# The passage from layer 0 to layer 1 in a four-layer graph kernel: halves of x moved up in two queues

## What is computed

```
x = _layernorm(x + _L0_gnn_ref(x, adj, ...), axis=-1)   # hypergraph convolution, 256 -> 512 -> 256
x = _layernorm(x + _L1_gnn_ref(x, adj, ...), axis=-1)   # q k v projection, scores, softmax
x = _layernorm(x + _L2_gnn_ref(x, adj, ...), axis=-1)
x = _layernorm(x + _L3_gnn_ref(x, adj, ...), axis=-1)
```

```
h = jax.nn.relu(hypergraph_conv(x, adj, W1, b1))
h = layer_norm(h, gamma, beta)
y = hypergraph_conv(h, adj, W2, b2)
return y + x
```

## Time and profile before

| | us |
|---|---|
| median of 3 runs (lowest to highest) | 689.02 (687.34 to 689.32) |
| the profiled execution, its own time | 687.93 |
| its span in the profile | 686.1 |
| PE busy | 628.5 (92%) |
| DVE busy | 564.2 (82%) |
| ACT busy | 525.1 (77%) |
| POOL busy | 372.5 (54%) |

### The profile page before, as it was taken

How to read it: one execution, slowest core, us unless ns; L and a number is a source line. 1 busy time by engine, 2 the same in 40 slices (tenths; PEclk the granted TensorE clock), 3 DMA queues, 4 the chain that set the end, 5 groups by cost and what they waited for, 6 DMA issues and landing times.

```text
span 686.1 us, 15857 instructions
## 1 busy us (share of the span) xinstructions
PE 628.5 (92%) x5014; PEld 453.4 (66%) x5014; DVE 564.2 (82%) x1712; ACT 525.1 (77%) x1191; POOL 372.5 (54%) x448
## 2 busy tenths in 40 slices
PE   5899999999999999879999799999999997999993
PEld 4577777777777776546666456665656664778783
DVE  3899988888888886758888858988888987688886
ACT  4667888777777787748888667877777875899995
POOL 1335556665555555756666414444434444798993
PEclk9999999999999999989999899999999999999998
DMA  9672438464544222545454324545454544378873
GB/s 276 182 210 56 88 71 223 82 160 95 140 121 96 63 32 32 93 95 95 91 92 93 61 63 79 105 86 103 84 103 81 105 85 71 69 176 188 183 188 124
DMA packets 174466, 76.14 MB, mean 111 GB/s; under 512 B 122160, under 2 KB 173872, under 8 KB 174384
## 3 DMA queue, kind: packets, MB, share of 16 engines
q1 hardware_dynamic: 164208, 66.34, 41.9%
q0 software_dynamic: 8448, 8.39, 8.3%
q10 hardware_dynamic: 1728, 0.40, 0.3%
HBM read 28.97 MB, written 8.39 MB: 54 GB/s over the span
## 4 chain that ended last, share of the span: by engine, by line
PE 25%; DVE 10%; POOL 6%; DMA 5%; issue 4%; ACT 2%; DVEq 0%; ACTq 0%; POOLq 0%
PE banks L86 8%; PE banks L88 7%; PE banks L87 7%; DVE l_st L1044 4%; DMA xT_lo<-x_halves 3%; POOL x_halves L1130 2%; POOL l_rstd L1069 2%; DMA l_TT_lo<-l_T_lo 2%; POOL l_U L1961 1%; PE banks L1224 1%; PE banks L1554 1%; DVE l_mid_lo L1716 1%; POOL l_T_lo L1758 1%; PE banks L1236 1%; PE banks L1832 1%
## 5 line engine op out<-in xcount | busy, mean ns | idle before, releaser
L1078 ACT ACTIVATE x_resident<-l_pre,l_nmr,l_rstd 128x256 f32<-128x256 f32 x256 | 142.3, 608 | 19.7 <-POOL l_nmr L1072 19.7
L973 POOL TENSOR_TENSOR hq<-hq 128x512 f32<-128x512 f32 x48 | 69.5, 1447 | 94.0 <-ACT hq L690 91.7
L1130 POOL TENSOR_TENSOR x_halves<-x_resident,x_halves 128x1024 f16<-128x1024 f32 x46 | 98.0, 2131 | 25.5 <-DVE l_pre L1307 22.3
L1044 DVE BATCH_NORM_STATS2 l_st<-l_pre 128x6 f32<-128x256 f32 x256 | 93.4, 411 | 0.0
L86 PE MATMUL banks<-Wk_lo,xT_hi 128*128 128x258 f16 (+1 forms) x256 | 84.5, 330 | 0.6 <-DVE l_far_lo L1709 0.3
L87 PE MATMUL banks<-Wk_hi,xT_lo 128*128 128x258 f16 (+1 forms) x256 | 84.5, 330 | 0.0
L88 PE MATMUL banks<-Wk_hi,xT_hi 128*128 128x258 f16 (+1 forms) x256 | 84.4, 330 | 0.0
L1069 POOL TENSOR_TENSOR l_rstd<-l_veps,minus_half 128x4 f32<-128x4 f32 x64 | 70.5, 1102 | 11.8 <-DVE l_veps L1058 6.2
L86 PE MATMUL banks<-W2T_lo,h_hi 128*128 128x257 f16 x256 | 70.8, 277 | 5.3 <-ACT zf L702 4.5
L88 PE MATMUL banks<-W2T_hi,h_hi 128*128 128x257 f16 x256 | 70.9, 277 | 0.0
L87 PE MATMUL banks<-W2T_hi,h_lo 128*128 128x257 f16 x256 | 70.7, 276 | 0.0
(11 more groups left out here) (200 smaller groups left out, 1942.7 us busy)
## 6 DMA issues: line engine op xcount, KB each, us to landing
adj<-in_adj SPq DMA_DIRECT2D x32, 256.0 KB, 3.6
x_halves<-in_x SPq DMA_DIRECT2D x16, 512.0 KB, 4.3
x_resident<-b_half SPq DMA_DIRECT2D x8, 1024.0 KB, 7.7
x_resident<-in_x POOLq DMA_DIRECT2D x16, 512.0 KB, 6.0
out<-x_resident SPq DMA_DIRECT2D x15, 512.0 KB, 3.2
x_resident<-in_L_gnn_W SPq DMA_DIRECT2D x2, 512.0 KB, 5.7
x_resident<-in_L_gnn_Wk SPq DMA_DIRECT2D x1, 768.0 KB, 9.2
xT_hi<-x_halves SPq DMA_TRANSPOSE x48, 3.2
```

Of the source, the lines that this page charges most:

```text
L973: pool.tensor_tensor(hq[:, 0, :], hq[:, 0, :], hq[:, h, :], ALU.add).then_inc(hqs_ok, 1)
L1044: dve.bn_stats(L.st[p][:, j, :], L.pre[p][:, j, :]).then_inc(L.st_ok, 1)
L1078: act.activation(K.x[:, gcols(g, j)], L.pre[p][:, j, :], ACT.Identity, bias=L.nmr[p][:, j:j + 1], scale=L.rstd[p][:, j:j + 1]).then_inc(L. ...
L1130: pool.tensor_tensor(F.xs[p][1], x_group(K, g), F.xs[p][0], ALU.subtract).then_inc(F.x_lo, 1)
```

## The change

ACT: `first_high(0)` stands in the step of group 14 and `first_high(1)` in the step of group 15, both beside `copy_z` of graph 3 of the group before. In the step of group 15 `copy_z` of graph 0 stands ahead of the four `norm_apply`, graph 1 between them, graph 2 behind them, and `squares_high` follows in the next step. POOL: `first_low(0)` and `first_low(1)` stand behind `hidden_power` in the steps of groups 12 and 13. In the step of group 14 `norm_scales` stands behind `hidden_power`. The seam's word 'nnno' puts three steps of layer 1, with the low halves of its groups 2 and 3, ahead of POOL's last step of layer 0, whose work is `norm_scales` of group 15. PE, DVE and SP keep their order, and no instruction is added or taken out.

```diff
-SEAMS_POOL = ('ooooo', 'ooon', 'ooonnn')
+SEAMS_POOL = ('nnno', 'ooon', 'ooonnn')
...
# layer 0, ACT, step
-            if has(-1):
+            if has(-1) and g < G:
                 copy_z(g - 1, 1)
+            if has(-1):
                 copy_z(g - 1, 2)
...
-            if has(-1):
+            if g == G - 2:
+                first_high(0)
+            if has(-1) and g < G:
                 copy_z(g - 1, 3)
+            if g == G - 1:
+                first_high(1)
+            if g == G:
+                squares_high(G - 1)
+                copy_z(G - 1, 3)
...
-            if isinstance(g, int) and g == G - 1:
-                first_high(0)
-                first_high(1)
+            if g == G - 1:
+                copy_z(G - 1, 0)
             if has(-2):
                 norm_apply(K, L, act, g - 2, p, 0)
                 norm_apply(K, L, act, g - 2, p, 1)
+            if g == G - 1:
+                copy_z(G - 1, 1)
+            if has(-2):
                 norm_apply(K, L, act, g - 2, p, 2)
                 norm_apply(K, L, act, g - 2, p, 3)
-            if has(0):
+            if has(0) and g < G - 1:
                 copy_z(g, 0)
                 squares_high(g)
...
# layer 0, POOL, step
-            if isinstance(g, int) and g == G - 2:
-                first_low(0)
-                first_low(1)
...
-            if has(0):
+            if has(0) and g != G - 2:
                 norm_scales(K, L, pool, g, p)
             if has(1):
                 hidden_power(g + 1)
+            if g == G - 2:
+                norm_scales(K, L, pool, g, p)
+            if g == G - 4:
+                first_low(0)
+            if g == G - 3:
+                first_low(1)
```

More of the change, by code:

```diff
@@ L735, in step @@
             once(g, 0, W.high_w2, act)
+            if has(-1) and g < G:
+                copy_z(g - 1, 1)
             if has(-1):
-                copy_z(g - 1, 1)
                 copy_z(g - 1, 2)
```

## The result

The changed kernel takes 685.33 us (median of 11 runs, 682.47 to 687.60), the kernel before 689.02 (11 runs). The ratio is 0.9945, with a 95% interval of 0.9927 to 0.9964: 0.55% faster. The profiled execution took 683.69 us, its span is 681.9, its mean clock 0.988 (before: 687.93, 686.1 and 0.981).

What follows compares the result with a forecast made beforehand. PE was taken as the bound in layer 0 (163.50 of 166.00 us busy), so only its waits could be won: +2.7 + 0 - 0.4 - 2.1 - 2.7 = -2.5 us, 685.4 from 687.93, median 686.5; range 682.6 to 691.3.

Steps and rivals of the forecast that it cites:

- First low half of group 0: Layer 0, behind zrs of group 13: POOL's low half delays DVE's `zn` and `h_lo`; PE loses 2.7 us (bounds 1.0 to 5.3).
- The first step: At zrs of group 13, POOL goes on with the low half until 255.1, so DVE's `zn` is 1.85 us late.
- gets in ahead of `h_lo` 1: POOL's sum of squares (1.32 us) runs between DVE's `h_lo` 0 and `h_lo` 1, which then ends near 260.5.
- Group 15: End of layer 0: PE's 2.54 us wait won on ACT, given back on DVE (0); sums of squares 0.4 us earlier.
- The forecast's bound on that side: Group 15's projections, if DVE is not held at all: 2.65 us won.
- Low transpose of group 2, with the swap: Layer 1: transpose issued at 293.2, not 295.45; PE goes on at 297.4, not 299.49: 2.1 us won (bounds 0.5, 3.55).
- The slow stretch: Layer 1, behind the low-transpose wait: PE's matmuls at 1.2 GHz until 304.91 return to full clock, 2.7 us won or 0.
- DVE is hardly held: Rival: DVE keeps the port, POOL's sums wait; 1.7 us lost once, squares 2.2 won, -5.3 in all, 683.7 us; chance 0.22.

Runs made afterwards that it cites:

- e5: The changed kernel with `first_low(0)` moved behind the third sum of squares in POOL's step of group 12; 683.40 us, ratio 0.9916 to the kernel before.
- e2: The changed kernel with all of POOL as in the kernel before, so ACT's part alone; 690.39 us, ratio 1.0024 to the kernel before.
- e4: The changed kernel with both first low halves back at the head of POOL's step of group 14; 686.67 us, ratio 0.9972 to the kernel before.
- e3: The changed kernel with `norm_scales` of group 14 ahead of `hidden_power` again; 683.20 us, ratio 0.9913 to the kernel before.
- e13: The changed kernel with POOL's seam word back from 'nnno' to 'ooooo'; 683.92 us, ratio 0.9914 to the kernel before.
- e7: The changed kernel with `first_low` replaced by a POOL memset to zero that reads nothing from SBUF; 683.50 us, ratio 0.9923 to the kernel before.
- e6: The changed kernel with DVE's softmax of group 1 ahead of `norm_variance` of group 0 in layer 1; 684.57 us, ratio 0.9947 to the kernel before.
- e9: The changed kernel with the edits of e3, e5 and e6 together; 681.38 us, ratio 0.9895 to the kernel before.
- e1: The kernel before with only POOL's seam word changed, 'ooooo' to 'nnno'; 683.64 us, ratio 0.9926 to the kernel before.

## Why the prediction was right, and where it was not

The forecast was 686.5, the result 685.33; the gain was forecast as 2.5 in the profiled execution and is 4.24 there. By its own terms, over the passage:

- **First low half of group 0: +2.7 forecast, +1.34 measured.** The first step was right: `rcs_lo` lasted 1.97, `zn` came 1.8 us late. The step that failed is that POOL's sum of squares "gets in ahead of `h_lo` 1". It did not: DVE, with its instructions back to back, kept going, and the sum lasted 2.66. Only the last `h_lo` was held (1.16 instead of 0.69), behind one with an input in PSUM (`l_pre` of 259.86). e5 shows that this one low half makes the term: with it later, the loss is gone.
- **Group 15: 0 and -0.4 forecast, -2.42 measured.** The same failed step, made a second time. `zn` was not held longer than its own low half, three `h_lo` took 1.88 again (the rows at 274.13 are like those at 258.05), and PE went on with a wait of 0.34. The copies were in time. The forecast's bound on that side was -2.65; it lay there. That ACT's 2.54 us are won only together with POOL's earlier low halves is what e2 and e4 show (3.98 and 3.97 us of wait without them); the prediction's mechanism has both in place and is not touched by it. Part of the gain is clock: from 250 to 285 it is 1.00, and was 0.95 with the wait of 2.54.
- **Low transpose of group 2, with the swap: -2.1 forecast, -2.42 measured.** In the whole change both parts came as said: PE waits 1.63 at the second projection (forecast 1.35 and 0.3), without the swap that wait is gone (e3), and the transpose goes out 2.06 us earlier against the square sums. But less hangs on the earlier transpose than the prediction had it: without the word (e13) the segment is 14.27, so 1.18 of the 2.42 comes anyway, 0.95 of it by the unexplained shorter landing.
- **The slow stretch: -2.7 forecast, -2.7 found.** The clock is 1.00. It is so in e13 too: what this term needs is that the wait of 3.55 is gone or split, not that the word does it. The segment shows only -1.13, because 1.58 was lost in it to a wait not forecast: 1.79 at 303.03 instead of 0.21.
- **What was missed: +1.58.** The prediction followed the low halves of groups 0 to 3, not that of group 4, which the word also moves up, onto the norm instructions ahead of the softmax. The rule was at hand (`l_dd` of the earlier trace rows).

Sum: +1.34 - 2.42 - 2.42 - 2.7 + 1.58 = -4.62. Two terms were too dark by 1.4 and 2.0, one of 1.6 was missing. The point came close partly because these errors have opposite signs. Of the rivals, "DVE is hardly held" has the mechanism of the first two terms: its 1.7 lost and 2.2 won stand against 1.34 and 2.42 measured. By its reckoning the time is 683.7, with the missed wait 685.3. I had given it a chance of 0.22, and kept 0.38 for my own. So the number of the forecast is good in part by luck. The rule that I leaned on (Trainium skill, SBUF — State Buffer, "Who interferes with whom": the first takes the shared ports for the whole instruction) agrees with the 1.97 and the 2.06; it says of one pair of instructions who waits, and I had made of it a turn for POOL between two of DVE's, from one pair at 52.44. What the prediction could not see from one trace is that the word and the rest remove the same wait (e13).

## What to carry to other kernels

Run each part of such a change by itself, and the change without it: here one word of a table gave all of the gain, everything but the word gave as much, the part on ACT alone was a loss, and two parts paid for the same wait. A large wait of PE has more than one cause queued behind it, so ask which engine would be late next (POOL's 4.21 us behind ACT's 2.54) before costing its removal, and split waits rather than gather them, since the clock fell behind those of 3.5 us and more in every passage profiled here, and only behind some of the shorter ones. An instruction that looks as if it stood in the way of an urgent one may be the cover for a round trip to another engine: moving the norm behind the softmax in all steps cost 1.1 us each.

## What the runs showed of the hardware that was not expected

- POOL can be the one that stands still: beside three back-to-back `h_lo` a sum of squares lasted 2.66 us, not 1.32 (a second one, at 274.90, lasted 2.25). At 52.44 POOL had got in between two instructions of DVE. What decides between the two I did not find out.
- A fill by POOL that reads nothing held a DVE cast of 4 elements a partition for 0.98 us instead of 0.17, and did not hold `zn` with its two inputs in SBUF (e7).
- Not only instructions with two tensors as inputs are held: `l_wn`, a TENSOR_SCALAR on 4x128 f32, lasted 1.03 us instead of 0.27 beside a low half (e6).
- The clock of 0.50 came behind a wait of 1.83 us in e7 and behind 1.56 in e9 (0.50 from 310 to 312), but not behind the same 1.56 in e6 (1.00 from 308 to 316), nor behind 1.79 in the changed kernel or 1.77 at 34.62 before. The length of the last wait alone does not tell.
- From SP's issue of the low transpose to PE's start it took 4.04 us before, 3.15 in e1 and 3.09 in e13, for the same transfer. None of the runs was made to separate this.
